# Attention: three of four key steps of the denominator added on GpSimd, the fourth by an adding transfer, over a ring of five probability buffers

## The reference, cut to what matters

```python
h = _sln(hidden, w, ln_g, ln_b, Wg, bg, Wb, bb)
qkv = (h @ Wqkv.T + bqkv).reshape(B, N, num_heads, hd, 3)
energy = jnp.einsum('bhqd,bhkd->bhqk', q, k)
att = jax.nn.softmax(energy, axis=-1) / D ** 0.5
out = jnp.einsum('bhqk,bhkd->bhqd', att, v)
out = jnp.moveaxis(out, 1, 2).reshape(B, N, D)
out = out @ Wp.T + bp
```

## Time and profile before

| | us |
|---|---|
| median of 3 runs | 1861.26 (1860.9 to 1867.59) |
| the profiled execution, its own time | 1867.83 |
| its span | 1865.7 |

### The profile page before, as it was taken

How to read it: one execution, slowest core, us unless ns; L and a number is a source line. 1 busy time by engine, 2 the same in 40 slices (tenths; PEclk the granted TensorE clock), 3 DMA queues, 4 the chain that set the end, 5 groups by cost and what they waited for, 6 DMA issues and landing times. The chain is left out here.

```text
span 1865.7 us, 27084 instructions
## 1 busy us (share of the span) xinstructions
PE 1815.0 (97%) x9510; PEld 1214.0 (65%) x9510; DVE 1252.1 (67%) x1986; ACT 836.4 (45%) x1547; POOL 1217.5 (65%) x681
## 2 busy tenths in 40 slices
PE   8999999999999999999999999999999999999897
PEld 4678888888888788888555545554555555454376
DVE  4655655655655565556887777777777777777387
ACT  3223123122223122221476666666666666666465
POOL 2665465465464243332588888888988888898565
PEclk9999999999999999999999999999999999999999
DMA  7410110210103657595877778777878787865796
GB/s 271 118 35 23 57 34 22 56 34 22 56 1 118 209 206 244 180 292 181 199 164 175 184 167 184 175 181 177 182 179 185 172 182 170 185 153 133 232 383 235
DMA packets 135373, 287.10 MB, mean 154 GB/s; under 512 B 23984, under 2 KB 41520, under 8 KB 127200
## 3 DMA queue, kind: packets, MB, share of 16 engines
q1 hardware_dynamic: 102996, 200.10, 35.8%
q0 software_dynamic: 9264, 66.11, 17.4%
q10 hardware_dynamic: 23008, 19.54, 3.3%
HBM read 134.68 MB, written 84.19 MB: 117 GB/s over the span
## 5 line engine op out<-in xcount | busy, mean ns | idle before, releaser
L1619 DVE TENSOR_REDUCE at_mrow<-banks 128x1 f32<-128x512 f32 x976 | 594.1, 681 | 163.7 <-PE banks L1465 163.6
L1715 POOL TENSOR_TENSOR at_sums<-at_probs 128x2048 f32<-128x2048 f32 x127 | 596.6, 4698 | 91.5 <-DMA at_sums<-at_sums 80.2
L1599 ACT ACTIVATE at_probs<-banks 128x512 f32<-128x512 f32 x1024 | 519.7, 621 | 182.7 <-PE banks L1483 177.4
L1465 PE MATMUL banks<-early_ks,early_qs 96*128 96x512 f32 x976 | 407.9, 418 | 11.0 <-DVE at_mrow L1619 7.1
L1483 PE MATMUL banks<-early_qs,early_ks 98*128 98x512 f32 x1024 | 408.0, 417 | 1.8 <-ACT at_probs L1599 1.8
L1465 PEld LDWEIGHTS banks<-early_ks,early_qs 96*128 96x128 f32 x976 | 184.8, 189 | 145.1 <-DVE at_mrow L1619 91.6
L1483 PEld LDWEIGHTS banks<-early_qs,early_ks 98*128 98x128 f32 x1024 | 193.7, 190 | 105.6 <-ACT at_probs L1599 81.5
L1495 PE MATMUL banks<-at_probs,at_v 128*32 128x512 f32 x2048 | 249.1, 603 | 0.7 <-DMA at_v<-v_scratch 0.7
L66 PE MATMUL banks<-l_nt,l_weights 128*128 128x512 f32 x768 | 179.4, 394 | 5.4 <-DVEq L1193 4.3
L66 PE MATMUL banks<-l_ht,l_weights 128*128 128x512 f32 x768 | 178.9, 393 | 1.9 <-issue 1.9
L657 ACT ACTIVATE l_gt<-banks,mod 128x512 f32<-128x512 f32 x60 | 45.1, 778 | 299.3 <-PE banks L526 263.5
(11 more groups left out here) (147 smaller groups left out, 2155.3 us busy)
## 6 DMA issues: line engine op xcount, KB each, us to landing
at_sums<-at_sums POOLq DMA_DIRECT2D x63, 1024.0 KB, 8.3
qk_scratch<-qk_out SPq DMA_DIRECT2D x64, 512.0 KB, 6.1
early_ks<-qk_scratch SPq DMA_DIRECT2D x48, 512.0 KB, 5.2
early_qs<-qk_scratch SPq DMA_DIRECT2D x96, 256.0 KB, 5.7
attn_scratch<-at_out SPq DMA_DIRECT2D x32, 512.0 KB, 7.5
o_a<-attn_scratch SPq DMA_DIRECT2D x32, 512.0 KB, 14.5
chunk_in<-x SPq DMA_DIRECT2D x8, 1024.0 KB, 5.4
v_scratch<-qk_v ACTq DMA_DIRECT2D x32, 256.0 KB, 3.0
```

Of the source, the lines that this page charges most:

```text
L1465: pe.matmul(em[n % 3][:], qs[0:96, slot, half, j, c * P:(c + 1) * P], ks[0:96, slot, j, keys * CH:(keys + 1) * CH], start=True, stop=True) ...
L1599: nc.scalar.activation(probs[:, i % 4, j, :], et[n % 3][:], ACT.Exp).then_inc(exp_done, 1)
L1619: nc.vector.tensor_reduce(mrow[:, half, keys, u:u + 1], em[n % 3][:], AX.X, ALU.max).then_inc(max_done, 1)
L1715: nc.gpsimd.tensor_tensor(into, probs[:, a], probs[:, a + 1], ALU.add).then_inc(pair_ready, 1)
```

## The change

The ring of probabilities gets a fifth buffer (`PROBS_RING`, `slot_of`), `sums` loses its third. POOL adds steps 0 and 1 of a quad into `sums[quad % 2]` as before, then adds step 2 to that in place, and the transfer adds step 3 straight from `probs`. The second addition no longer waits for a transfer; the issue of the transfer waits for the last one. ACT may fill a slot again when `av` and either the addition or the transfer that reads it are done. `multiply`, `round_off` and `remain` go one pair later on POOL (P1, P2, P3), and both `store`s go later in SP's queue: behind `widen_rden` instead of ahead of `place_neg`.

```diff
+        PROBS_RING = 5
-        probs = sb("at_probs", [P, 4, HG, CH])
-        sums = sb("at_sums", [P, 3, HG, CH])
+        probs = sb("at_probs", [P, PROBS_RING, HG, CH])
+        sums = sb("at_sums", [P, 2, HG, CH])
...
+        def slot_of(g, i):
+
+            return (STEPS * g + i) % PROBS_RING
...
                 if not first:
                     spread_den(g - 1, 1)
-                    store(g - 1, 0)
                 place_neg(g, slot, 1)
                 if not first:
                     widen_rden(g - 1, 1)
+                    store(g - 1, 0)
                 fetch(1)
                 fetch(2)
                 spread_den(g, 0)
-                if not first:
-                    store(g - 1, 1)
                 if with_next:
                     place_neg(g + 1, (slot + 1) % RING, 0)
                 widen_rden(g, 0)
+                if not first:
+                    store(g - 1, 1)
                 fetch(3)
...
-                    if not (first and i < 4):
-
-                        act.wait_ge(av_done, STEPS * g + i - 3)
-                        act.wait_ge(pair_ready, PAIRS * g + (i - 4) // 2 + 1)
+                    if not (first and i < PROBS_RING):
+
+                        old = STEPS * g + i - PROBS_RING
+                        act.wait_ge(av_done, old + 1)
+                        if old % 4 == 3:
+                            act.wait_ge(quad_ready, 16 * (old // 4 + 1))
+                        else:
+                            act.wait_ge(pair_ready, 2 * (old // 4) + (1 if old % 4 < 2 else 2))
...
-                            if pair == SPAN * half:
+                            if pair == SPAN * half + 1:
                                 multiply(g - 1, half)
-                            if pair == SPAN * half + 1:
+                            if pair == SPAN * half + 2:
                                 round_off(g - 1, half)
-                            if pair == SPAN * half + 2:
+                            if pair == SPAN * half + 3:
                                 remain(g - 1, half)
 
                     quad, second = divmod(PAIRS * g + pair, 2)
-                    pool.wait_ge(exp_done, HG * (STEPS * g + 2 * pair + 2))
-                    if second and quad >= 1:
-
-                        pool.wait_ge(quad_ready, 16 * quad)
-                    if not second and quad >= 2:
-
-                        pool.wait_ge(den_done, quad - 1)
-                    into, a = sums[:, 2 if second else quad % 2], 2 * pair % 4
-                    nc.gpsimd.tensor_tensor(into, probs[:, a], probs[:, a + 1], ALU.add).then_inc(pair_ready, 1)
-                    if second:
+                    total = sums[:, quad % 2]
+                    i = 2 * pair
+                    if not second:
+
+                        pool.wait_ge(exp_done, HG * (STEPS * g + i + 2))
+                        if quad >= 2:
+
+                            pool.wait_ge(den_done, quad - 1)
+                        nc.gpsimd.tensor_tensor(total, probs[:, slot_of(g, i)], probs[:, slot_of(g, i + 1)], ALU.add).then_inc(pair_ready, 1)
+                    else:
+
+                        pool.wait_ge(exp_done, HG * (STEPS * g + i + 1))
+                        pool.wait_ge(pair_ready, PAIRS * g + pair)
+                        nc.gpsimd.tensor_tensor(total, total, probs[:, slot_of(g, i)], ALU.add).then_inc(pair_ready, 1)
+                        pool.wait_ge(exp_done, HG * (STEPS * g + i + 2))
                         pool.wait_ge(pair_ready, PAIRS * g + pair + 1)
-                        pool.dma_start(sums[:, quad % 2].rearrange("p j c -> p (j c)"), into.rearrange("p j c -> p (j c)"),
+                        if quad >= 1:
+
+                            pool.wait_ge(quad_ready, 16 * quad)
+                        pool.dma_start(total.rearrange("p j c -> p (j c)"), probs[:, slot_of(g, i + 1)].rearrange("p j c -> p (j c)"),
                                        accum_op=ALU.add).then_inc(quad_ready, 16)
```

More of the change, by code:

```diff
@@ L1494, in av @@
                     rows = slice(HD * j, HD * (j + 1))
-                    last = pe.matmul(av_ps[rows, :], v[:, slot, kc, rows], probs[:, kc % 4, j, :],
+                    last = pe.matmul(av_ps[rows, :], v[:, slot, kc, rows], probs[:, slot_of(g, i), j, :],
                                      start=kc == 0, stop=kc == KC - 1)
@@ L1557, in _ @@
             pe.wait_ge(pair_ready, PAIRS * G - 1)
-            tiles = [sums[:, (QUADS * G - 1) % 2], probs[:, 2], probs[:, 3]]
+            tiles = [sums[:, (QUADS * G - 1) % 2]] + [probs[:, slot_of(G, i)] for i in (-2, -1)]
             for tile in tiles:
@@ L1598, in group @@
                         act.wait_ge(et_done, n + 1)
-                        nc.scalar.activation(probs[:, i % 4, j, :], et[n % 3][:], ACT.Exp).then_inc(exp_done, 1)
+                        nc.scalar.activation(probs[:, slot_of(g, i), j, :], et[n % 3][:], ACT.Exp).then_inc(exp_done, 1)
                     if g == 1 and i % KC in (3, 5):
@@ L1724, in _ @@
             groups(pool, group)
+            remain(G - 2, 1)
             multiply(G - 1, 0)
```

## The result

The changed kernel took **1879.21 us** (median of six runs, 1875.02 to 1887.51), the kernel before 1863.31 beside it (six runs). The ratio is 1.0087, 95% interval 1.0073 to 1.0101. The forecast of 1850 was wrong in sign, and the time lies outside its range of 1840 to 1867. The profiled execution is the longest of the six: 1887.51 us for a span of 1885.4, with a mean granted clock of 0.987. What its trace shows is thus the change at its costliest, 8 us above the median.

A forecast was written before the change was run, and what follows sets the result against it. The prediction took a loop of PE and ACT as the bound, with 22.1 us above its floor. 22.1 - 9.8 (DVE's waits) - 0.5 (tail) = 11.8 us off; against the median of 1861.26 it forecast 1850, range 1840 to 1867.

The forecast's parts named there:

- What the stores meet: Moved stores fly with the next load and q1's transfer, taken as 8.5 us, landing 10.0 into the next half.
- the rule weighed there: DMA engines take turns between queues, so q1's transfer would share turns with store and load; spoke against the change, unpriced.
- The store's head start: In SP's queue: the store, starting at about 26 into the half, leads q1's transfer (issued at 27.7) by 1.7 us.
- P3's 0.58: Excess of a half's last pair over its floor, in us, from transfers in flight together; both parts were to go.
- the 20.3 us of DVE's waits: DVE's waits for the spread denominators, said to stay; 9.8 of the 22.1 us above the floor were left for them.
- Rival 2: Collision costs more than before: P1's denominator product late if q1 flies above 9.5 us; +12.6 us, 1874; chance 0.14.
- Taking the store out of q0's stretch: Store leaves the flight of q0, maxima and denominators: q0 lands at 23.3, maxima 1.5 us earlier.
- the forecast of 11.8 us off: Whole kernel: net gain summed as 22.1 - 9.8 - 0.5 = 11.8 us.
- The floor of 25.87: Shortest half of the attention stage, in us, set by a loop of PE and ACT that the change leaves alone.
- 22.1 us: Attention stage's time above the floor over 28 halves, 0.79 a half; the most that rearranging POOL's work could give.
- The tail: PE's 3.62 us wait before the projection's second chunk, its loads behind one more store: +0.5 us, bounds 0 and 2.
- the earlier issue of q1: POOL's second addition no longer waits for q0's landing, so q1's transfer is issued at 27.7 instead of 29.3, 1.6 earlier.

The follow-up runs named there:

- experiment 4: Changed kernel, with the store and the 512 KB load issued between the write of the inverted denominators and the wait for its landing: 1849.76 us, 0.9908.
- experiment 6: Changed kernel with only the store issued ahead of the wait for the inverted denominators, the 512 KB load behind their broadcast: 1851.25 us, 0.9921.
- experiment 7: Changed kernel with only the 512 KB load issued ahead of the wait for the inverted denominators, the store behind their broadcast: 1849.81 us, 0.9915.
- experiment 9: Experiment 6 plus 26 memory-to-memory copies of 512 KB, one behind each 512 KB load of groups 2 to 14: 1886.96 us, 1.0112.
- experiment 2: Changed kernel with stores and small operations back at their old places; additions, ring of five and transfer as changed: 1880.40 us, 1.0074.
- experiment 12: Experiment 2 with the multiplication moved to P1 and the rounding to P2, beside the subtraction: 1861.80 us, 0.9990.
- experiment 5: Kernel before (old additions, four buffers) with the order of SP's queue from experiment 4: 1852.60 us, 0.9934.
- experiment 11: Experiment 8's program once more, five rounds on another chip, against the kernel before: 1846.61 us, 0.9887.
- Experiment 8: Experiment 4 with multiplication, rounding and subtraction back in their old pairs P0, P1, P2: 1845.40 us, 0.9890.
- experiment 10: Changed kernel with the spread denominators issued ahead of the 1.28 MB of loads: 1964.26 us, 1.0544.

## Why the prediction was wrong

**The step that failed** is "What the stores meet". It took 8.5 us for q1's transfer, by analogy with a q0 that had no store beside it, although the rule weighed there spoke against it. Measured are 10.9 and 9.8 us at the two ends of the half shown, landing at 11.9 and 11.4 rather than 10.0, and 9.8 in the median of all q1. Experiments 4, 6, 7 and 9 show the reason: with one companion of 512 KB, started some 2 us ahead, nothing is lost; with two it is. The store's head start, taken as 1.7 us, was 0.34 and 1.2. It was worked out with denominators that come back 2.4 us earlier, and in the half shown they came back as late as before (the broadcast starts 25.8 in, before 25.9), with the loads behind q1 2.0 us later (11.9 in, before 9.9). (By its own rows the working gives 25.9 - 2.4 + 1.7 = 25.2 for the store, a head start of 2.5, and not the "about 26" that it wrote.) The terms that hung on it failed with it: P3's 0.58 didn't go, and the 20.3 us of DVE's waits, said to stay, became 34.7. The Trainium skill, "DMA: Bandwidth & Descriptors", section on queues, rings and completion order, says that an engine takes turns between queues; the trace agrees, with 6.9 us for q1 where store and load have landed before it is issued (experiment 4) and 9.8 to 10.9 where they fly beside it.

**What I had as a rival.** Rival 2 named this place (P1's product), this point (a flight of q1 above 9.5) and the sign, with 1874. It had 0.14. Its sum, P1 late and P3 above the floor as before, is what the 26 ordinary halves show (P1 0.27 and P3 0.70 a half; by its sum 0.7 and 0.6). The reason for its P3 was another: the store has left q0's stretch, but the late load slows q0 instead, so that q0 lands at 25.3 in the half shown, where the forecast had 23.3. And it lacked the step after, that the spread denominators can fall behind q0's transfer. In the profiled execution that happened in two halves and made 18 of the 43.6 us above the floor. That these halves come from the crossing of the two issues (15.1 and 15.3 against 15.0) is read from the trace; in the other halves the denominators went out at 14.4 or earlier.

**What held.** POOL's waits for the adding transfer vanished, as forecast, and so did PE's waits for the maxima. Issue times were 15.0 and, outside the long halves, 27.8 to 29.1 (forecast 14.8 and 27.7). Taking the store out of q0's stretch is worth what was forecast for it or more: experiment 6 does this and leaves q1 the company that it had, and its ratio is 0.9921, where the forecast of 11.8 us off stood for 0.9937. The in-place addition costs the same as the other (4.57 us in the median against 4.58). The floor of 25.87 held in every variant, and 22.1 us was the right ceiling: experiment 4 left 4.5 of it. The tail, priced at +0.5, was no loss: PE's wait ahead of the second chunk went from 3.62 to 2.66.

**What I costed at nothing and was not nothing:** the earlier issue of q1. By itself (experiment 2) it collides with the broadcast and costs 0.7%, unless the multiplication moves as well (experiment 12). I had priced the small operations' move only by the issue of q0, where it leaves a gain of 0.2 us. Experiments 5 and 11 differ only in the fifth buffer and the additions, and their intervals don't overlap: these are worth 0.5% once the stores are out of the way. (Experiment 8, the same program as 11 with fewer runs, has the same ratio, but its interval touches that of experiment 5.)

**Open:** I followed the lateness from half to half (load, denominators, store), but no run set off the chain by itself. The trace fits it: of the 28 halves 24 lie above the floor. Two of the four on it come before the first store (984.9 us), and the other two follow the long halves; in all four the q1 that P1's product reads flew 7.0 or 7.1 us. How the harm divides between the number of companions and their head start is not measured. How often the long half occurs in an execution is known for the profiled ones alone.

## What to carry to other kernels

When a transfer is moved out of a crowded stretch, list what flies in the stretch that receives it, and take the flight of the critical transfer from a row with that much company; moving it into a stretch in which its queue waits for a landing (here 22.8 to 24.2 into the half) made the kernel 0.9% faster than before. A queue worked in order turns a late landing into later loads and later small transfers, so a price for the first delay alone is too low. And a stall of PE behind which the granted clock falls costs more than its length: here 5.2 us became 8.6.

## What the runs showed of the hardware

An adding transfer of 1 MB from on-chip to on-chip memory landed in 6.9 us at the least, in experiment 4 with nothing large beside it at its start, and in up to 12.9 us with loads beside it (the longest of experiment 10). A transfer of 8 KB that is issued just behind one came in only when it was nearly done: in the half at 1255.70 the spread denominators were issued at 1270.79, 0.11 behind q0's transfer, which flew 10.4 us, and released DVE at 1280.76, 10.0 us later.
